# New piece times for three phases of a decoder kernel, cross attention 2's scores in fewer matmuls, and its output bias added elsewhere

## The reference

```python
x = LN(x + L0_attn(x))            # 16 heads of 16, Fourier bias, causal
x = LN(x + L0_xattn(ctx, ctx, x)) # 16 heads, 64 keys, float mask * -1e9
x = LN(x + L0_moe(x))             # 8 experts of 128, the top 2, and 2 shared ones
x = LN(x + L1_attn(x))            # low-rank q, k, v (latent 64), 16 heads, causal, bias
x = LN(x + L1_xattn(x, ctx))      # one head of 256, below
x = LN(x + L1_ffn(x))             # 1024 wide, relu(h + phase * sin(theta + 0.1 h) ...)

def L1_xattn(q, k, mask):                      # "cross attention 2"
    qh, kh = q @ Wq + bq, k @ Wk + bk
    vh = kh @ Wv + bv
    scores = where(mask == 0, -10000.0, qh @ kh.T)
    return softmax(scores) @ vh @ Wo + bo
```

## Time and profile before

| | us |
|---|---|
| median of three | 3624.97 |
| the three | 3624.97, 3619.38, 3625.34 |
| profiled execution, its own time | 3628.03 |
| its span | 3626.1 |

### The profile page before, as it was taken

One profiled execution on the slowest core, in us unless ns is written; L12 is line 12 of the kernel. 1 busy time (PEld: TensorE's weight loads), 2 busy tenths in 40 slices (PEclk: granted clock), 3 DMA queues, 4 the chain that ended last, 5 costly groups with the idle time before them and its releaser, 6 DMA issues.

```text
span 3626.1 us, 59862 instructions
## 1 busy us (share of the span) xinstructions
PE 3344.5 (92%) x20706; PEld 2528.1 (70%) x20706; DVE 2625.4 (72%) x7153; ACT 2283.5 (63%) x4067; POOL 1022.4 (28%) x1576
## 2 busy tenths in 40 slices
PE   5999999999999848999999999999999876999998
PEld 4677777777777636777777777777777655766664
DVE  5688888888888644677777777777777534788876
ACT  3677777777777622456666555556556543677776
POOL 2244444444444422222222322222223110000000
PEclk8999999999999979999999999999999877999999
DMA  7654545445544021444444444444444421011010
GB/s 193 101 95 84 88 96 107 84 88 95 107 84 82 17 82 53 84 80 77 86 92 94 94 88 88 90 89 93 92 87 88 73 44 62 12 36 35 25 35 24
DMA packets 203403, 283.27 MB, mean 78 GB/s; under 512 B 48929, under 2 KB 131874, under 8 KB 194274
## 3 DMA queue, kind: packets, MB, share of 16 engines
q1 hardware_dynamic: 203106, 279.46, 38.2%
HBM read 179.49 MB, written 96.73 MB: 76 GB/s over the span
## 4 chain that ended last, share of the span: by engine, by line
PE 71%; ACT 11%; DVE 7%; DMA 5%; issue 4%; SPq 1%; POOL 1%; PEld 0%; POOLq 0%; ACTq 0%; PEldq 0%; DVEq 0%
PE ps L829 35%; PE ps L1003 8%; PE ps L978 7%; PE ps L1201 5%; PE ps L1017 5%; ACT q_stack L1669 5%; PE ps L953 3%; DMA qk_scratch<-parts 3%; ACT pt L1686 2%; PE ps L984 1%; PE ps L1077 1%; PE ps L888 1%; PE ps L1028 1%; DMA k_stack<-qk_scratch 1%; DVE nmax L1351 1%
## 5 line engine op out<-in xcount | busy, mean ns | idle before, releaser
L1686 ACT ACTIVATE pt<-ps 128x512 f32<-128x512 f32 x1280 | 735.9, 598 | 346.7 <-PE ps L1003 338.8
L1889 POOL TENSOR_SCALAR_AFFINE_SELECT pt<-pt 128x256 f32<-128x256 f32 x1024 | 392.1, 419 | 704.9 <-ACT pt L1686 704.9
L978 PE MATMUL ps<-k_stack,q_stack 96*128 96x512 f32 (+3 forms) x2048 | 547.2, 338 | 42.3 <-ACT q_stack L1669 11.8
L1358 DVE CUSTOM_DVE_ANT_0 ps<-ps,future 128x512 f32<-128x512 f32 (+3 forms) x1024 | 481.7, 515 | 141.9 <-PE ps L978 138.8
L1003 PE MATMUL ps<-q_stack,k_stack 100*128 100x512 f32 (+3 forms) x2048 | 538.6, 345 | 29.3 <-ACT q_stack L1669 23.4
L1003 PEld LDWEIGHTS ps<-q_stack,k_stack 100*128 100x128 f32 x2048 | 351.5, 195 | 124.9 <-ACT q_stack L1669 37.2
L978 PEld LDWEIGHTS ps<-k_stack,q_stack 96*128 96x128 f32 x2048 | 355.6, 194 | 103.2 <-ACT q_stack L1669 18.8
L1351 DVE TENSOR_REDUCE nmax<-ps 128x1 f32<-128x512 f32 (+2 forms) x768 | 354.4, 502 | 92.0 <-PE ps L984 91.0
L1895 POOL TENSOR_TENSOR rs<-rs 128x4 f32<-128x4 f32 x96 | 97.1, 1012 | 1062.0 <-DVE rs L1394 1062.0
L1669 ACT ACTIVATE q_stack<-ps 4x512 fp32r<-4x512 f32 x512 | 300.8, 588 | 64.7 <-PE ps L992 56.5
L1017 PE MATMUL ps<-pt,v_ones 128*32 128x512 f32 (+3 forms) x4096 | 312.1, 446 | 5.7 <-POOL pt L1889 5.3
(11 more groups left out here) (278 smaller groups left out, 7958.6 us busy)
## 6 DMA issues: line engine op xcount, KB each, us to landing
qk_scratch<-parts SPq DMA_DIRECT2D x64, 1024.0 KB, 5.5
q_stack<-qk_scratch SPq DMA_DIRECT2D x384, 128.0 KB, 4.9
k_stack<-qk_scratch SPq DMA_DIRECT2D x384, 128.0 KB, 5.6
gate_of<-gate_scratch SPq DMA_DIRECT2D x128, 256.0 KB, 5.6
x_mid<-x_ring SPq DMA_DIRECT2D x32, 512.0 KB, 3.9
x_ring<-x_mid SPq DMA_DIRECT2D x32, 512.0 KB, 5.3
x_ring<-in_x SPq DMA_DIRECT2D x16, 512.0 KB, 3.8
out_dram<-x_ring SPq DMA_DIRECT2D x16, 512.0 KB, 2.9
```

Of the source, the lines that this page charges most:

```text
L978: done = e.matmul(bank(bank_of[piece])[:, at:at + width], a.q[0:96, base + h, t * P:(t + 1) * P], a.k[0:96, base + h, 0:width], start=a.la ...
L1358: done = e.tensor_tensor_reduce(src, src, future[:, SEQ - width:SEQ], -1.0, 3e38, ALU.add, ALU.min, nmax[:, g % 2, to:to + 1])
L1686: e.activation(dst, src, ACT.Exp).then_inc(exp_up.sem)
L1889: done = e.affine_select(out=blk, in_=blk, compare_op=ALU.is_ge, fill=0.0, base=0, pattern=[[0, 2], [1, P]], channel_multiplier=-1)
```

## The change

1. The planned times of all three phases are new. Periods: 70.45 to 73.001, 91.45 to 93.878 and 31.45 to 32.104. In phase 1 the order is nearly as it was (PE: 24 of 1968 pieces move by one place, ACT: 4, DVE, POOL and SP: none), the banks differ. In phase 2 PE has 286 of 2320 pieces in another place (by at most 4), ACT 582 of 1376, DVE 421 of 1392, POOL 28 of 304, SP 130 of 272. Among them: `send(n+1,0)` now before `rows(n,3)` on SP; on DVE `h3(n,6)` before the maximum of `S(n+16,3,2)`, and `gt` before that of `S(n,0,9)`; on PE `dn(n,1,0)` and two scores before `up(n,2,0)`, `N(n,0)` behind a `PV` and `T(n,0,0)` behind `dn(n,0,0)`. In phase 3 the order and the banks are the same, but for the new piece on POOL.
2. Cross attention 2's scores: `a_h` and `a_l` lie beside each other in `a_parts`, so that `ch` meets both in one matmul of 128 columns and `cl` meets `a_h` in one of 64: 16 matmuls instead of 24. DVE copies the second half out of PSUM and adds it to the first. The query bias is folded into `offset` (formerly `unseen`) in the prologue, by two multiplications and two additions of 128x512 on DVE; the two ACT copies go.
3. `co_b` is no longer added in `cw` (two fp32 matmul records of 1x128 by 1x256 go, and `ones`). It is loaded to 128 partitions (128 KB instead of 1) and added to `x` by POOL in a new piece `tb x1`, behind `tc x1`.

```diff
 TABLE = {
-    1: (70.45, {
+    1: (73.001, {
...
-    2: (91.45, {
+    2: (93.878, {
+        "sync": {
+            "send": [81.126, 103.751],
+            "rows": [112.729, 134.367, 157.237, 181.687],
...
-        "sync": {
-            "send": [76.442, 95.983],
-            "rows": [97.435, 117.928, 140.108, 160.952],
...
         "vector": {
-            "gt": [-47.732],
-            "h3": [-47.625, -31.127, -24.632, -21.3, -6.146, 7.033, 19.611, 23.072, 28.061, 40.153],
...
+            "gt": [-52.06],
+            "h3": [-48.276, -39.818, -29.766, -23.058, -9.447, 1.716, 10.509, 16.97, 24.019, 34.808],
...
-    3: (31.45, {
+    3: (32.104, {
...
         "gpsimd": {
+            "tb x1": [-29.775],
+            "ln x1": [-6.654],
...
         put("tc", "x1", b)
+        put("tb", "x1", b)
...
-        a_h, a_l = (sb(st3, f"a_{part}", [P, CT, keys_all], F32R) for part in "hl")
+        a_parts = sb(st3, "a_parts", [P, CT, BATCH, 2, CTX], F32R)
...
-        LN_BIAS = {"x0": xo_b, "a1": proj_b}
+        LN_BIAS = {"x0": xo_b, "a1": proj_b, "x1": co_b}
...
-                    ops.append((ones[:, :], co_b[:, :]))
                     product(e, bank(bank_of[piece])[:, 0:DIM], ops).then_inc(cw_up.sem)
...
-                        ops = []
-                        for c in range(CT):
-                            ops += three(ch[:, c, rows], cl[:, c, rows], a_h[:, c, keys], a_l[:, c, keys])
-                        done = product(e, bank(bank_of[piece])[:, t * CTX:(t + 1) * CTX], ops)
+                        both = bank(bank_of[piece])[:, 2 * t * CTX:2 * (t + 1) * CTX]
+                        done = None
+                        for c, part in ((0, ch), (0, cl), (1, cl), (1, ch)):
+                            wide = part is ch
+                            done = e.matmul(both if wide else both[:, 0:CTX], part[:, c, rows],
+                                            a_parts[:, c, b, :, :].rearrange("p a k -> p (a k)") if wide else a_parts[:, c, b, 0, :],
+                                            start=wide and c == 0, stop=wide and c == 1)
...
+                        for n in range(2):
+                            cols = slice(n * 512, n * 512 + 512)
+                            e.wait_ge(bq_up, n + 1)
+                            e.wait_ge(keys_lo, 12)
+                            e.tensor_tensor(tile32[:, n, :], bank(4 + n), seen[:, cols], ALU.mult).then_inc(mine.up())
+                            e.wait_ge(*mine.now)
+                            e.tensor_tensor(offset[:, cols], offset[:, cols], tile32[:, n, :], ALU.add).then_inc(mine.up())
...
-                    e.tensor_tensor(sc3[:, :, :], bank(bank_of[piece])[:, 0:TT * CTX].rearrange("p (t k) -> p t k", t=TT),
-                                    key_row(q_bias), ALU.add).then_inc(cs_add.sem)
+                    halves = bank(bank_of[piece]).rearrange("p (t a k) -> p t a k", t=TT, a=2)
+                    e.tensor_copy(sx3[:, :, :], halves[:, :, 1, :]).then_inc(mine.up())
+                    e.wait_ge(*mine.now)
+                    e.tensor_tensor(sc3[:, :, :], halves[:, :, 0, :], sx3[:, :, :], ALU.add).then_inc(cs_add.sem)
...
-                        for n in range(2):
-                            e.wait_ge(bq_up, n + 1)
-                            e.activation(q_bias[:, n * 512:n * 512 + 512], bank(4 + n), ACT.Copy)
...
-                        e.dma_start(co_b[:, :], dram["co_b"].partition_broadcast(1)).then_inc(mask_in3, 16)
+                        e.dma_start(co_b[:, :], dram["co_b"].partition_broadcast(P)).then_inc(mask_in3, 16)
```

More of the change, by code:

```diff
@@ L129 @@
 TABLE = {
-    1: (70.45, {
-        "tensor": {
[23 rows of a table removed]
+    1: (73.001, {
+        "sync": {
+            "ld 1": [-97.022],
+            "send": [-38.962, -17.925],
+            "rows": [-34.639, -20.46, -6.518, 9.743],
+            "st 1": [191.304],
+            "kl": [85.259],
+        },
+        "tensor": {
[23 rows of a table added]
         },
         "scalar": {
[17 rows of a table removed]
[17 rows of a table added]
         },
         "vector": {
[18 rows of a table removed]
[18 rows of a table added]
         },
         "gpsimd": {
[L196 to L202, removed]
-        "sync": {
[L204 to L208, removed]
-        },
-    }),
@@ L211 @@
-    2: (91.45, {
-        "tensor": {
[25 rows of a table removed]
+            "sel": [33.846, 39.483, 50.296, 53.398, 62.817, 67.168, 80.089, 84.087],
+            "ln a0": [101.272],
+            "tb x0": [109.55],
+            "xs": [122.301, 127.992, 133.585, 138.71, 143.02, 148.536, 156.092, 158.515],
+            "xe": [128.982, 130.868, 137.351, 144.01, 146.514, 152.094, 159.523, 161.878],
+            "ln x0": [178.877],
+        },
+    }),
+    2: (93.878, {
+        "sync": {
+            "ld 2": [-86.634],
+            "send": [81.126, 103.751],
+            "rows": [112.729, 134.367, 157.237, 181.687],
+            "st 2": [286.011],
+            "gh": [-44.116],
+            "sg": [-42.66, -42.225, -30.954, -25.075, -10.139, -3.534, 5.404, 15.49],
+        },
+        "tensor": {
[25 rows of a table added]
@@ L296 @@
-    3: (31.45, {
-        "tensor": {
-            "cw": [-44.295],
-            "tc x1": [-28.819],
-            "cs": [-23.855],
-            "cp": [-16.754],
-            "tm co": [-13.994],
-            "tc ff": [5.095],
-            "fa": [37.798, 43.482, 44.899, 47.658, 51.853, 56.099, 58.583, 62.384],
-            "fd": [50.668, 53.858, 57, 60.143, 63.285, 66.771, 70.792, 72.518],
-            "bk 3": [77.556],
+            "tb a1": [68.891],
+            "sel": [153.931, 158.405, 174.807, 182.379, 203.121, 207.457, 224.119, 229.281],
@@ new lines @@
+            "ln a1": [282.211],
+            "h2": [None, None, -32.316, -26.437, -11.501, -7.068, 4.042, 14.128, 21.966, 29.062],
+            "ln ex": [50.931],
+        },
+    }),
+    3: (32.104, {
+        "sync": {
+            "ld 3": [-38.092],
+            "st 3": [87.457],
+        },
+        "tensor": {
+            "cw": [-46.056],
+            "tc x1": [-30.885],
+            "cs": [-25.97],
+            "cp": [-16.802],
+            "tm co": [-14.942],
+            "tc ff": [3.838],
+            "fa": [36.814, 43.475, 44.899, 47.842, 52.744, 55.915, 59.086, 62.256],
+            "fd": [50.998, 54.168, 57.339, 60.51, 63.68, 66.299, 72.086, 73.832],
+            "bk 3": [78.638],
@@ L307 @@
         },
         "scalar": {
[11 rows of a table removed]
[11 rows of a table added]
         },
         "vector": {
[L322 to L332 removed]
+            "cw": [-28.07],
@@ L333 @@
+            "tc x1": [-29.267],
+            "cs": [-24.039],
+            "ce": [-20.481],
+            "ln x1": [-10.11],
+            "lm x1": [-5.408],
+            "tc ff": [5.133],
+            "fa": [42.885, 47.029, 51.73, 52.642, 57.957, 60.21, 63.35, 64.68],
+            "fb": [45.636, 51.132, 53.485, 57.358, 59.611, 62.748, 65.848, 66.446],
+            "ln ff": [79.975],
+            "lm ff": [84.677],
         },
         "gpsimd": {
-            "ln x1": [-4.648],
-            "ln ff": [82.365],
-        },
@@ L338 @@
-        "sync": {
-            "ld 3": [-34.372],
-            "st 3": [85.767],
+            "tb x1": [-29.775],
+            "ln x1": [-6.654],
+            "ln ff": [83.431],
         },
@@ L743, in decoder @@
         cq_b, ck_b, cv_b = (sb(st3, f"{n}_cols", [P, CT]) for n in ("cq_b", "ck_b", "cv_b"))
-        co_b, f2_b = sb(st3, "co_b_row", [1, DIM]), sb(st3, "f2_b_cols", [P, CT])
-        ones = sb(st3, "ones", [1, P])
+        co_b, f2_b = sb(st3, "co_b_rows", [P, DIM]), sb(st3, "f2_b_cols", [P, CT])
         wf2 = sb(st3, "w_down", [P, FT, DIM])
         ff_c, fc = sb(st3, "ff_c", [P, 4 * FT]), sb(st3, "fc", [P, 12, FT])
-        a_h, a_l = (sb(st3, f"a_{part}", [P, CT, keys_all], F32R) for part in "hl")
+        a_parts = sb(st3, "a_parts", [P, CT, BATCH, 2, CTX], F32R)
         v_h, v_l = (sb(st3, f"v_{part}", [P, CT, BATCH, 2, CTX], F32R) for part in "hl")
-        q_bias, seen, unseen = (sb(st3, n, [P, keys_all]) for n in ("q_bias", "seen", "unseen"))
+        seen, offset = (sb(st3, n, [P, keys_all]) for n in ("seen", "offset"))
         W3 = Weights(st3, 3)
@@ L761, in decoder @@
         ch, cl = sb(st3, "xh3", [P, CT, SEQ], F32R), sb(st3, "xl3", [P, CT, SEQ], F32R)
-        sc3 = sb(st3, "sc3", [P, TT, CTX])
+        sc3, sx3 = sb(st3, "sc3", [P, TT, CTX]), sb(st3, "sx3", [P, TT, CTX])
         sm3 = sb(st3, "sm3", [P, 3, TT, 1])
@@ L1257, in vector @@
                         e.wait_ge(*mine.now)
-                        e.tensor_scalar(unseen[:, :], seen[:, :], 10000.0, -10000.0, ALU.mult, ALU.add)
+                        e.tensor_scalar(offset[:, :], seen[:, :], 10000.0, -10000.0, ALU.mult, ALU.add)
                         e.tensor_copy(bq[:, :, :], cq_b[:, :].unsqueeze(2).broadcast_to([P, CT, P])).then_inc(circle_up)
@@ L1282, in vector @@
                                 done.then_inc(keys_lo)
```

(27 more changed lines are left out.)

23 lines of the change are left out of this document (removed), and 258 rows, old and new, of the table TABLE.

## The result

The changed kernel takes 3635.46 us (median of 9 runs, 3628.25 to 3639.19) against 3624.41 (9 runs, 3619.30 to 3626.19): ratio 1.0032, 95% interval [1.0022, 1.0042]. Forecast were 3594 and a range of 3576 to 3614. The profiled execution took 3639.19, span 3637.5, against 3628.03 and 3626.1.

A forecast was written before the change was run, and what follows sets the result against it. TensorE was taken to set the pace in every phase. Phase 1 +17, phase 2 −31, phase 3 −20 and its prologue +3 sum to −31: 3597 against the profiled execution, 3594 as median; range 3576 to 3614.

The forecast's parts named there:

- Phase 1, +17: Phase 1, `tm v0`: other banks make PE wait 1.22 us for DVE's later mask addition, 14 times: +17 us.
- Rival A: Phase 1: the added wait is swallowed by PE's idle time, giving 3577 us; chance 0.2.
- Against it stands what the new order makes late: Phase 2: `gt` before `S(n,0,9)` on DVE delays PE by 0 to 0.15 us a tile, −2 us of the gain.
- rival C: Phase 2: `gt` before `S(n,0,9)` makes PE wait 2.95 us in each of 14 tiles, giving 3637 us; chance 0.05.
- The term for `q_stack`, 0.97: Phase 2: PE's `q_stack` wait goes whole because `send(n+1,0)` is issued before `rows(n,3)`, saving 0.97 us a tile.
- The term for `hid_l`, 0.99 and a part of 0.25: Phase 2: `h3` before `S` on DVE removes the `hid_l` wait, 0.99 us a tile; 0.25 more for empty-pipe starts after waits.
- rival B: Phase 2: idle time only moves on, 3625 us, half of it 3610; chance 0.12 for none or nearly none, 0.2 for half.
- `tb x1`, "Nothing": Phase 3: the new POOL addition takes 2.39 us but stands 19.7 us before `ln x1` needs it, so costs nothing.
- cs and co_b, −0.86 and −0.83: Phase 3, PE: fewer `cs` matmuls save 0.86 us a tile, removing the two `co_b` records saves 0.83.
- Rival D: Phase 3: the 128-column matmuls run at four passes, 0.213 us each, so `cs` wins nothing: 3608 us; chance 0.08.
- The give-back of 0.47: Phase 3: PE comes 0.83 us earlier, DVE 0.43 later by its copy; with 0.79 slack, `fa(n,6)` waits 0.47 a tile.
- The prologue, +2.9: Phase 3's prologue: four more 128x512 instructions on DVE, the last engine at the barrier, cost +2.9 us.

The follow-up runs named there:

- v0_bank: Changed kernel, all times kept, banks of `xs(b,7)` and `xp(b,5)` exchanged in phase 1: 3616.05 us, ratio 0.9978 to the kernel before.
- send_first: Changed kernel with old times in phases 1 and 2, plus `send(n+1,0)` ahead of `rows(n,3)` on the DMA queue: 3604.53 us, ratio 0.9949 to the kernel before.
- cs_only: Kernel before with 16 score matmuls, DVE's copy and the prologue bias, `co_b` still by matmul, no `tb x1`: 3618.56 us, ratio 0.9976.

## Why the prediction was wrong

- **Phase 1, +17:** right, in mechanism, place and size. 1.12 us of recorded wait in 14 tiles, a period longer by 1.29 (1.22 forecast), +16.1 at the phase's end; v0_bank shows it to be that one bank. Rival A is out.
- **Phase 2, "Against it stands what the new order makes late": this is the step that failed.** I put what becomes late at 0 to 0.15 us a tile, having looked only at `gt` on DVE and, on the DMA queue, only at what `send(n+1,0)` passes. The same queue also had `sg(·,2)` and `rows(·,2)` exchanged, and `sg(·,7)` and `rows(·,0)`. The first costs in every tile by a slower landing, the second at the phase's start. Both are shown: 21 us came back by these two alone, a part of them by the clock that no longer fell behind the long wait, which the prediction had no term for either. Beside it stand new waits of 0.2 us for `el`, and `gt` before `S(n,0,9)` (rival C) cost nothing that the table of waits shows.
- **The term for `q_stack`, 0.97:** mis-sized. The earlier trace rows give the sum of two causes: the landing, and a rest of 0.3 at each of the 24 waits (7.1 us in send_first, where nothing waits for a landing). That the rest comes from `N`, `mr` and `T` following each other too closely on PE is my reading and was not tried. The send alone was worth 0.32 a tile of period. The trace before had it: the first wait of a tile is between 0.28 and 1.24 us, 0.28 to 0.31 in five of the twelve tiles, and the second never above 0.29. Only the spread was the landing's.
- **The term for `hid_l`, 0.99 and a part of 0.25:** right, 1.29 by itself.
- **The half that rival B gave** (3610) is what happened in kind, "the idle time only moves on", and in size it went further: 30.6 to 19.0 us of idle time, a period shorter by only 0.6, and the two ends of the phase longer by 12.6.
- **The ends of the phases:** I multiplied by 14 and 16 tiles and gave the first and last ones no price. In phase 3 the first tiles are a chain over DVE and ACT, with PE waiting, and PE's savings don't count: −1.20 came in 12 tiles, −14.4 instead of −20.
- **`tb x1`, "Nothing":** right in the steady tiles, wrong in the first two. There PE's wait for `lm x1` before the next transposes is 3.76 and 3.98 us; before, and in cs_only, which has no `tb x1`, it is 1.68 and 1.84. The link is in the traces. The last DVE instruction of `ln x1`, 128x4 with both inputs in SBUF, starts 0.07 us after POOL began the `tb x1` of the next tile, and lasts until that one is over: 2.30 us in place of 0.16. ACT's `lm x1` waits for it, and PE for ACT. Below are the wait, POOL and DVE of the changed kernel, and the same DVE instruction in cs_only.
```profile
3095.78 1.97 PE L954 MATMUL ps<-ident,x_ring 128*128 128x128 f32 x8 [3.76 <-ACT x_ring L1727]
3091.25 2.34 POOL L1893 TENSOR_TENSOR x_ring<-x_ring,co_b_rows 128x1024 f32<-128x1024 f32 x1
3091.32 2.30 DVE L1410 SCALAR_TENSOR_TENSOR rs<-ag,rs 128x4 f32<-128x4 f32 x1 [1.13 <-POOL rs L1907]
...
3070.00 0.16 DVE L1411 SCALAR_TENSOR_TENSOR rs<-ag,rs 128x4 f32<-128x4 f32 x1 [1.19 <-POOL rs L1910]
```
  So the exclusion of GpSimd and DVE that the prediction names is real here: it holds up two tiles in every kernel with `tb x1` and none in the kernel before and cs_only, at 2.1 us each. In the steady tiles no DVE instruction beside a `tb x1` is longer than elsewhere, and the 0.7 a tile is not there: the period is 1.20 shorter, 1.22 was forecast without it. Behind the 3.76 us PE again works at a granted clock of 0.50, from 3095.78 to at least 3103 us.
- **cs and co_b, −0.86 and −0.83:** right to 0.01 (2.59 to 1.73, 2.89 to 2.07). For `cs` there is some luck in it: the 1.79 that I said I took would save 0.80, and 0.86 belongs to the lower bound, which came. Rival D is out: the eight matmuls of 128 columns take 0.11 to 0.14 us of the stream each, not 0.213. The give-back of 0.47 is right as a sum (0.86 + 0.82 − 1.20 = 0.48), but only 0.16 of it is at `fa 6`, where I had put it all; most is at `bk 3`.
- **The prologue, +2.9:** 3.4 in the wait at the barrier. The ledger's +4.7 at the first `fa` also holds `tb x1`'s two times 2.1; what stands against them there was not taken apart.

Put together: 16.1 + 7.8 − 7.4 + 4.8 + 4.7 − 14.4 = +11.6 against +17 − 31 + 3 − 20 = −31, and 36 of the 43 us between them are phase 2's.

## What to carry to other kernels

A reordered queue has to be read whole, piece by piece against the old one, not only at the exchange one is looking for: two neighbours that change places on a DMA queue can cost as much as the stalls which the reordering was made for, and one long wait of TensorE is paid twice, the second time in matmuls at the lower clock. Before a measured wait is counted as a gain, split it by tile: the part that is the same in every tile has another cause than the part that varies, and stays. And a saving per tile counts only in tiles where its engine sets the pace; the first and last tiles get a line of their own, where savings are worth nothing and added latencies count in full, as `tb x1` showed. When a planner's times are replaced to mend two stalls, try the two swaps alone first: here they won 21 us, and the new times of phases 1 and 2 lost 24 (3635 against 3611).

## What the runs showed of the hardware

A 256 KB broadcast to 128 partitions, issued 0.4 us ahead of six 128 KB transfers, delayed the landing of the last of them from 6.9 to 9.9 us after its issue; cut to 64 KB it left 7.6. I had taken the landing of a transfer to hang on its own size and on its place in the queue.

Matmuls in fp32r with 128 stationary columns took 0.108 us of the stream on average, whether all 24 had 64 moving columns (2.59 us) or 8 of 16 had 128 (1.73 us).

A GpSimd addition of 128x1024 that read SBUF held a DVE instruction of 128x4 with both inputs in SBUF for its whole length, 2.30 us in place of 0.16, when the DVE one started 0.07 us after it.

After PE had idled 5.6 to 5.8 us at the start of phase 2, its granted clock was 0.50 for the next 6 us of matmuls and then 1.00; after idling 1.1 us at the same place it stayed 1.00.
